# Feed-forward weights made beside the cross attentions, and transposed probabilities copied by halves of the keys

## The reference

```python
for layer in (0, 1):
    x = x + cross_attention(norm(x), ctx_1024, mask if layer == 0 else None)   # 16 heads of 16
    x = x + (linear_attention if layer == 0 else causal_attention)(norm(x))    # over the 64 latents
    x = x + (int8_ffn if layer == 0 else fp4_ffn)(norm(x))

def cross_attention(q, kv, mask):
    q, k, v = heads(q @ Wq.T + bq), heads(kv @ Wk.T + bk), heads(kv @ Wv.T + bv)
    p = softmax(q @ k.T / 4 + mask * -1e9)
    return merge(p @ v) @ Wo.T + bo

def ffn(x):                       # 256 -> 704 -> 256, weights quantised on the chip
    h = silu(quant(x) @ quant(w_gate).T) * (quant(x) @ quant(w_up).T)
    return quant(h) @ quant(w_down).T
# int8: weights by rows, w / (max|w| / 127) rounded; activations by one scale.
# fp4:  blocks of 16, w / (max|w| / 6) rounded to {0, .5, 1, 1.5, 2, 3, 4, 6}, times the scale.
```

## Time and profile before

| | |
|---|---|
| median of 3 runs | 1437.82 us (1437.0 to 1437.97) |
| the profiled execution | 1439.74 us, its span 1437.8 us |
| busy, of the span | PE 1300.0, PEld 895.3, DVE 939.4, ACT 784.8, POOL 656.6 us |
| mean granted TensorE clock | 0.955 of 2.4 GHz |

### The profile page before, as it was taken

How to read it: one execution, slowest core, us unless ns; L and a number is a source line. 1 busy time by engine, 2 the same in 40 slices (tenths; PEclk the granted TensorE clock), 3 DMA queues, 4 the chain that set the end, 5 groups by cost and what they waited for, 6 DMA issues and landing times. The chain is left out here.

```text
span 1437.8 us, 27154 instructions
## 1 busy us (share of the span) xinstructions
PE 1300.0 (90%) x10721; PEld 895.3 (62%) x10722; DVE 939.4 (65%) x1670; ACT 784.8 (55%) x1315; POOL 656.6 (46%) x351
## 2 busy tenths in 40 slices
PE   6999999999999966965599999999999997897697
PEld 3676676666666644642256666766667665696465
DVE  4656655666556755957657768676566566586886
ACT  4675666666666623534366666666666664354311
POOL 2755566656666522400145556565555555440200
PEclk9999999999999988987699999999999998899798
DMA  4221111211111030000210100200010000000000
GB/s 159 76 58 45 45 45 45 87 47 45 45 45 45 1 102 0 1 1 0 108 37 31 51 30 31 80 31 31 31 59 31 31 1 24 4 1 1 0 11 19
DMA packets 17085, 55.29 MB, mean 38 GB/s; under 512 B 2753, under 2 KB 8897, under 8 KB 12737
## 3 DMA queue, kind: packets, MB, share of 16 engines
q1 hardware_dynamic: 16960, 53.56, 11.4%
HBM read 52.51 MB, written 1.05 MB: 37 GB/s over the span
## 5 line engine op out<-in xcount | busy, mean ns | idle before, releaser
L429 POOL TENSOR_TENSOR ca_prob<-ca_prob,ca_inv_sum 128x1024 f32<-128x1024 f32 x256 | 493.4, 1948 | 378.4 <-DVE ca_inv_sum L707 378.4
L608 ACT ACTIVATE ca_kT<-bank,ca_bk 64x512 f32<-64x512 f32 x256 | 174.6, 682 | 223.4 <-PE bank L465 221.6
L512 PEld LDWEIGHTS bank<-ident,ca_prob 128*128 128x128 f32 x2048 | 238.4, 141 | 89.4 <-issue 65.7
L512 PE MATMUL bank<-ident,ca_prob 128*128 128x128 f32 x2048 | 266.7, 274 | 9.0 <-POOL ca_prob L429 7.0
L465 PE MATMUL bank<-ca_ctxT,ca_wk 128*128 128x512 f32 x512 | 244.4, 602 | 17.4 <-DMA ca_bk<-in_L_xattn_bk 17.4
L477 PE MATMUL bank<-ca_wv,ca_ctxT 128*128 128x256 f32 x1024 | 254.5, 392 | 0.0
L684 DVE CUSTOM_DVE_ANT_0 ca_neg_logit<-bank,ca_mask_add 128x1024 f32<-128x1024 f32 x128 | 151.6, 1222 | 131.6 <-PE bank L502 95.0
L477 PEld LDWEIGHTS bank<-ca_wv,ca_ctxT 128*128 128x128 f32 x1024 | 184.6, 190 | 82.2 <-issue 62.5
L687 DVE TENSOR_REDUCE ca_neg_max<-bank 128x1 f32<-128x1024 f32 x128 | 150.7, 1219 | 103.3 <-PE bank L502 103.3
L630 ACT ACTIVATE ca_prob<-ca_neg_logit,ca_neg_max 128x1024 f32<-128x1024 f32 x128 | 146.9, 1150 | 62.8 <-DVE ca_neg_max L684 62.8
L630 ACT ACTIVATE ca_prob<-bank,ca_neg_max 128x1024 f32<-128x1024 f32 x128 | 142.5, 1114 | 63.8 <-DVE ca_neg_max L687 63.8
(11 more groups left out here) (278 smaller groups left out, 1333.9 us busy)
## 6 DMA issues: line engine op xcount, KB each, us to landing
ca_ctxT<-in_ctxT SPq DMA_DIRECT2D x32, 1024.0 KB, 5.0
ca_mask_i<-in_mask SPq DMA_DIRECT2D x32, 256.0 KB, 6.4
lat<-in_x SPq DMA_DIRECT2D x1, 1024.0 KB, 4.9
out<-lat SPq DMA_DIRECT2D x8, 128.0 KB, 1.9
la_w_qkv<-in_L_attn_w_qkv SPq DMA_DIRECT2D x1, 768.0 KB, 3.9
la_w_down<-in_L_ffn_w_down SPq DMA_DIRECT2D x1, 704.0 KB, 8.0
ca_fw_raw<-in_L_ffn_w_down SPq DMA_DIRECT2D x1, 704.0 KB, 4.3
la_w_gate<-in_L_ffn_w_gate SPq DMA_DIRECT2D x1, 640.0 KB, 5.7
```

The costliest lines, as they stand in the source:

```text
L429: pool.tensor_tensor(prob[:, x, :], prob[:, x, :], inv_sum[:, x:x + 1].broadcast_to([P, CTX]), ALU.mult).then_inc(norm_ready, 1)
L512: tr = pe.transpose(bank[:, x, n * P:(n + 1) * P], prob[:, 2 * (s % 2) + p, (4 * h + n) * P:(4 * h + n + 1) * P], core.ident[:, :])
L608: op = act.activation(kT[half * S:(half + 1) * S, b % 2, 2 * m + r, :], bank[r * S:(r + 1) * S, x, :], ACT.Identity, bias=bk[r * S:(r + 1) ...
```

## The change

- **Copies by halves.** `take_t` becomes `take_t_on_vector(s - 1, 0)` and `take_t_on_scalar(s - 1, 1)`: VectorE copies half h = 0 of both pairs, ScalarE half h = 1 of both. The places in the lists stay.
- **Int8 weights in the first cross attention.** Raw weights are loaded one matrix at a time into one buffer. VectorE quantises each in five steps (from s = 4, 16, 28), TensorE transposes it in three units of four transposes (from s = 10, 22, 34), each into one bank of the pool, and ScalarE copies each unit out in two instructions. The linear attention loses that work, the int8 feed-forward its transposes and copies.
- **Fp4 weights in the second.** VectorE's eight steps start at s = 4, 20, 36 and leave the grid in f32 in the raw buffer, POOL multiplies by the scales at s = 12, 28, 44, TensorE transposes in units from s = 14, 30, 46, ScalarE copies. The fp4 feed-forward starts with the layer norm alone.
- **Memory and order.** q4 and attnT have half their size: the second half of the queries is projected at s = 28 and 29 in place of 8 and 12, when the first has been used, and attnT goes round over four batches. The mask is loaded into one buffer, not two, after the one before is converted. `queries` comes two steps later (s % 4 == 2). The bf16 identity is made before the first latents are transposed.
- The cross attention becomes a class `CrossAttention`, its plan of banks a class `Banks` with the same turn.

```diff
-        def take_t(eng, copy, s, p):
-            n = s // 2
-            j = 2 * (s % 2) + p
-            if n >= 2:
-                wait_filled(eng, ("pv", n - 2))
-            for h in range(2):
-                x = wait_filled(eng, ("t", s, p, h))
-                copy(probT[:, n % 2, 4 * h:4 * h + 4, j, :],
-                     bank[:, x, :].rearrange("p (n q) -> p n q", q=P)).then_inc(taken[x], 1)
+    def take_t_on_scalar(self, act, s, h):
+        n = s // 2
+        if n >= 2:
+            self.banks.wait_filled(act, ("pv", n - 2))
+        for p in range(2):
+            x = self.banks.wait_filled(act, ("t", s, p, h))
+            self.banks.free(act.activation(self.probT[:, n % 2, 4 * h:4 * h + 4, 2 * (s % 2) + p, :],
+                                           self.core.bank[:, x, :].rearrange("p (n q) -> p n q", q=P), ACT.Copy),
+                            ("t", s, p, h))
...
+class Banks:
+    def open(self, pe, key, bank=None):
+        if bank is None:
+            bank = 4 + self.turn % 4
+            self.turn += 1
+        wait(pe, self.taken[bank], self.count[bank])
+        self.count[bank] += 1
+        self.at[key] = (bank, self.count[bank])
+        return bank
...
 class Fp4Weights:
+    def scale_on_pool(self, pool, x):
+        pool.wait_ge(self.step, 8 * (x + 1))
+        grid, scale = fp4_scaled(self.raw[:, 0:self.blocks[x] * HD], self.scale[:, 0:self.blocks[x]], self.blocks[x])
+        pool.tensor_tensor(grid, grid, scale, ALU.mult).then_inc(self.scaled, 1)
+
+    def transposes_on_tensor(self, pe, x, i):
+        pe.wait_ge(self.scaled, x + 1)
+        b = self.banks.open(pe, ("w", x, i))
+        for c in (2 * i, 2 * i + 1):
+            r = self.ROWS[c]
+            for k in range(KD):
+                o = (c % 2 * KD + k) * P
+                if x < 2:
+                    tr = pe.transpose(self.core.bank[:, b, o:o + r], self.raw[0:r, c * D + k * P:c * D + (k + 1) * P],
+                                      self.core.ident[0:r, 0:r])
...
+class Int8Weights:
+    def step_on_vector(self, dve, x, n):
...
+        elif n == 3:
+            dve.wait_ge(self.step, 3 * x + 3)
+            for c in range(pieces):
+                dve.tensor_scalar(raw[:, c, :], raw[:, c, :], self.inv[:, c:c + 1], ROUND, ALU.mult, ALU.add)\
+                    .then_inc(self.rounded, 1)
+        else:
+            if x >= 1:
+                self.banks.wait_filled(dve, ("i", x - 1, self.UNITS - 1))
+            for c in range(pieces):
+                dve.wait_ge(self.rounded, first + c + 1)
+                dve.tensor_scalar(whole[:, c, :], raw[:, c, :], ROUND, None, ALU.subtract).then_inc(self.ready, 1)
...
+def first_layer(core, ffn_weights):          # second_cross alike, from FW_STEPS + 10
 (TensorE)
+                if 1 <= s <= STEPS:
+                    ca.transposes(pe, s - 1, 1)
+                for x in range(3):
+                    if 6 <= s - IW_STEPS[x] < 9:
+                        ffn_weights.transposes_on_tensor(pe, x, s - IW_STEPS[x] - 6)
+                if s in Q_STEPS:
+                    ca.project_q(pe, 1, Q_STEPS.index(s))
+                if s % 8 == 2 and s >= 10:
...
 (ScalarE)
+                if s < STEPS:
+                    ca.exponentials(act, s)
+                if s + 4 < STEPS:
+                    ca.take_k(act, s + 4)
+                if s >= 1:
+                    ca.take_t_on_scalar(act, s - 1, 1)
+                for x in range(3):
+                    if 6 <= s - IW_STEPS[x] < 9:
+                        ffn_weights.take_on_scalar(act, x, s - IW_STEPS[x] - 6)
...
 (VectorE)
+                if 1 <= s <= STEPS:
+                    ca.take_t_on_vector(dve, s - 1, 0)
+                if s < STEPS:
+                    ca.inverses(dve, s)
...
 (linear_attention, VectorE)
             ln.on_vector(dve)
-            ffn_weights.on_vector(dve)
             dve.wait_ge(w_loaded, 96)
...
 (fp4_ffn, POOL)
-            for x in range(3):
-                flat = wq[x][:, :, :].rearrange("p c n -> p (c n)").rearrange("p (n k) -> p n k", k=HD)
-                grid, scale = fp4_scaled(weights.grid[x][:, :], weights.scale[x][:, :], weights.blocks[x])
-                pool.tensor_tensor(flat, grid, scale, ALU.mult).then_inc(wq_ready, 1)
```

More of the change, by code:

```diff
@@ new lines, in take_on_scalar @@
+    def take_on_scalar(self, act, x, i):
+        b = self.banks.wait_filled(act, ("w", x, i))
+        for c in (2 * i, 2 * i + 1):
+            r = self.ROWS[c]
+            o = c % 2 * KD * P
+            if x < 2:
+                op = act.activation(self.wT[x][:, :, c * P:c * P + r],
+                                    self.core.bank[:, b, o:o + KD * P].rearrange("p (k q) -> p k q", q=P)[:, :, 0:r],
+                                    ACT.Copy)
+            else:
+                op = act.activation(self.wdT[0:r, c, :], self.core.bank[0:r, b, o:o + D], ACT.Copy)
+        self.banks.free(op, ("w", x, i))
@@ L242, with __init__ @@
 GROUPS = 4
 STEPS = B * GROUPS
-POOL_BANKS = (4, 5, 6, 7)
-Q_STEPS = (8, 12)
 HALF_CTX = CTX // 2
-class BankPlan:
-    def __init__(self):
-        self.uses = [0] * 8
+Q_STEPS = (28, 29)
+class Banks:
+    def __init__(self, core, sem):
+        self.core = core
+        self.filled = [sem(f"filled{n}") for n in range(8)]
+        self.taken = [sem(f"taken{n}") for n in range(8)]
+        self.count = [0] * 8
         self.at = {}
         self.turn = 0
[L257 to L263, removed]
@@ L298, in cross_attention, with done @@
[L298 to L303, removed]
+    def open(self, pe, key, bank=None):
[6 more added lines that the diff above has]
+        return bank
+    def done(self, instruction, key):
+        instruction.then_inc(self.filled[self.at[key][0]], 1)
@@ L304, in cross_attention @@
+IW_STEPS = (4, 16, 28)
+def first_layer(core, ffn_weights):
+    nc, d, bank = core.nc, core.dram, core.bank
     with ExitStack() as ctx:
         def sb(name, shape, dt=F32):
[L306 to L311, removed]
@@ L443, in _ @@
+            pool.wait_ge(ffn_weights.pad_set, 1)
+            pool.wait_ge(const_loaded, 64)
+            ca.queries(pool, 0)
+            ca.convert_mask(pool, 0)
+            ca.add_output_bias(pool)
             for s in range(STEPS):
-                normalise(s)
+                ca.normalise(pool, s)
                 if s % GROUPS == 0 and s // GROUPS + 1 < B:
-                    queries(s // GROUPS + 1)
-                    if masked:
-                        mask(s // GROUPS + 1)
-        @block.tensor
@@ new lines, in _ @@
+                    ca.convert_mask(pool, s // GROUPS + 1)
+                if s % GROUPS == 2 and s // GROUPS + 1 < B:
+                    ca.queries(pool, s // GROUPS + 1)
+        @block.scalar
+        def _(act):
+            ca.ln.on_scalar(act)
+            act.wait_ge(ca.wk_loaded, 32)
+            for n in range(4):
+                ca.take_k(act, n)
+            ca.take_latents_on_scalar(act)
+            act.wait_ge(ca.wq_loaded, 32)
+            ca.take_q_on_scalar(act, 0)
+            for s in range(STEPS + 1):
+                if s < STEPS:
+                    ca.exponentials(act, s)
+                if s + 4 < STEPS:
+                    ca.take_k(act, s + 4)
+                if s >= 1:
+                    ca.take_t_on_scalar(act, s - 1, 1)
+                for x in range(3):
+                    if 6 <= s - IW_STEPS[x] < 9:
+                        ffn_weights.take_on_scalar(act, x, s - IW_STEPS[x] - 6)
+                if s == Q_STEPS[0]:
+                    ca.take_q_on_scalar(act, 1)
@@ L1826, in _ @@
             down(TILES - 1)
-def cross(core, layer, ffn_weights=None):
-    with ExitStack() as ctx:
-        core.q4 = ctx.enter_context(core.nc.sbuf_tensor(f"q4_{layer}", [P, 4, B * S], F32))
-        core.attnT = ctx.enter_context(core.nc.sbuf_tensor(f"attnT{layer}", [P, KD, B * S], F32))
-        cross_attention(core, layer, layer == 0, layer == 0, ffn_weights)
 def perceiver(nc, dram, out):
```

1113 lines of the change are left out of this document (576 added, 537 removed).

## The result

| | before | after |
|---|---|---|
| median of 4 runs | 1437.41 us | 1529.66 us |
| lowest to highest | 1435.73 to 1437.97 | 1528.59 to 1531.32 |
| ratio, 95% interval | | 1.0642 [1.0629, 1.0655] |
| span of the profiled execution | 1437.8 | 1529.3 |

The change makes the kernel 92 us slower. The forecast was 1524, 5.7 us lower. The table gives the length of each stage, from the start of one layer norm to the next (rows L142), in the profiled executions. The third line has, for each stage, the forecast's terms.

A forecast was written before the change was run, and what follows sets the result against it. TensorE, full at 2.4 GHz in both cross attentions, was taken as the bound. Terms 75.1 + 6.8 + 3 + 4 + 10 - 8.4 - 4.0 = +86.5 on the profiled 1439.7, median 1.9 lower: 1524 us, range 1487 to 1552.

The forecast's parts named there:

- Copies by halves: Cross attentions: TensorE waits for ScalarE's t(p0,h1) copy behind take_k, 34 times 1.54 and 84 times 0.27 us: 75.1 us.
- the late inverse: Cross attention ends: VectorE's inverse, now behind a copy of the second transposes, delays POOL's normalisations: 3 us (1 to 6).
- rival A: Cross attentions: only the long bank waits bite, the 22.7 us of short ones go: 1490 us, chance 0.10.
- Weight units on TensorE: Both cross attentions: 36 weight transposes in each layer added to a full TensorE: 6.8 us (5 to 8).
- Ports in the second layer: Second cross attention: VectorE's two-input fp4 steps behind the inverse lengthen POOL's pair of normalisations: 4 us (0 to 7).
- Ports in the first layer: First cross attention: int8 steps of six short VectorE instructions beside POOL's normalisations: 10 us, between nothing and 19.
- Out of the linear attention: Linear attention: without 42 VectorE int8 weight instructions ahead of them, the first features run earlier: -8.4 us (-7 to -9).
- Out of the fp4 head: Fp4 feed-forward's layer norm: with POOL silent, L147 and L152 take 0.17 us each: -4.0 us (-3.5 to -4.2).
- B: Cross attentions: no bank wait, ScalarE's copy finishes before the next opener asks: 1434 us, faster, chance 0.07.
- C: Cross attentions: VectorE held by POOL in most weight steps, 19 us first layer, some 17 second: 1547 us, chance 0.13.
- D: Cross attentions: the copies balance but the ports don't, slower without a bank wait: 1449 us, chance 0.02.
- What was put at nothing: Half-size q4 and attnT, single mask buffer, later queries and weight loads, POOL's scale multiplications, early bf16 identity: no cost.

The follow-up runs named there:

- the fifth experiment: The changed kernel, halves kept, with each int8 rounding step one whole-width instruction in place of six: 1513.52 us, ratio 1.0532.
- pairs with one instruction: The changed kernel with copies by pairs again (VectorE pair 0, ScalarE pair 1) and int8 rounding steps as single instructions: 1430.96 us, ratio 0.9951.
- The third experiment: The changed kernel with ScalarE copying t(p1,h0's sibling) t(p1,h1) first and t(p0,h1) second: 1594.22 us, ratio 1.1092.
- the second experiment: The changed kernel, halves kept, with ScalarE copying t(p0,h1) before the key copies (take_k) and t(p1,h1) behind them: 1450.28 us, ratio 1.0101.
- the halves alone: The kernel before with only the copies split by halves, no weight work moved: 1503.48 us, ratio 1.0464.
- The last experiment: Pairs with one instruction, plus three POOL multiplications into an unread tile at the head of the fp4 feed-forward: 1438.61 us, ratio 1.0008.

## Why the prediction was right, point by point

The total is nearer than its parts. The first layer came out 8.4 us above its terms, the linear attention, int8 and fp4 stages together 4.9 below theirs, the causal attention 1.8 above. That these partly cancel is luck. The bounds 1508 to 1544 are also narrower than the terms' own bounds added up, which give some 1504 to 1549.

**Copies by halves (forecast 75.1): right in place, sort and size; the late inverse (3) right in place.** The cleanest measure is the difference between the fifth experiment and pairs with one instruction, in which nothing but the split differs: 1513.52 - 1430.96 = 82.6 us. The forecast has 75.1 + 3 + 4 = 82.1 for what hangs on it. Of that difference the waits for ScalarE's copies are 74.1 (70.1 - 2.8, and 34 x 0.2), those for POOL 2.0 (8.9 and 6.9). The rest is in no wait: TensorE's busy time, for the same 10722 matmuls, is 1301.8 against 1287.1, and without the loads' 6.8 that is 7.9 us of longer rows, not traced. So the large term is shown, and the other 7 only as a sum.

By stage it is 550.1 - 512.2 = 37.9 against 24.6 + 11.6 + 1.5 = 37.7 in the first, and 559.6 - 515.7 = 43.9 against 27.7 + 11.1 + 1.5 + 4 = 44.3 in the second. The third experiment shows that all the waits are there, the short ones too; that rules out rival A. The second shows that it is the order in one queue. The late inverse is seen in the halves alone, where the waits for POOL grew by 3.4 us (forecast 3). In the change they are 7.8, against 7.0 before: they stand at the stage ends, as said (4.0 between 500 and 573, 2.7 between 1240 and 1300), but nearer 1 us than 3 there.

**Weight units on TensorE (6.8): right,** 2.6 + 4.3 = 6.9 in pairs and one instruction.

**Ports in the second layer (4): nearer 2, and not shown apart.** The stage came out at +48.6 against +48.8, but the parts agree less well. In pairs and one instruction the second stage's +4.3 is no more than the units' 4.5. In the second experiment, where the bank waits are gone and the inverse is still late, it takes 518.8, +7.4: without the units 2.9 for the inverse and the ports together, where the forecast has 5.5. And in the halves alone the second layer loses 33.5 us and the first 30.8, with equal waits for ScalarE's copies; 2.7 is what the fp4 steps can have cost there. That the stage agrees to 0.2 is in part luck.

**Ports in the first layer (10, bounds 0 and 19): the term that was mis-sized.** From the stage's +58.4 the other terms take 24.6 + 11.6 + 2.3 + 1.5 = 40, which leaves 18.4; the fifth experiment took 17.9 off the stage.

It is the upper bound, and its mechanism was right: I had VectorE held for both normalisations and the maxima 4.8 late, and the trace has six instructions in 5.52 us and maxima 4.5 after the scores. Its sum was right partly by luck. It had six steps of six instructions, and the third matrix has two in each; and TensorE's waits for VectorE in this stage are 5.7 us for the value copy (L707) and 4.6 for the copy of the attention's output (L749), 9.6 more than before, not 19. Of the rest some 5 is the clock: it is 0.97 and 0.98 in the windows 60 to 160 and 160 to 260, and 1.00 in both in the fifth experiment.

Where I went wrong was in taking the middle between two rows. L177 in the earlier trace rows, which goes first and holds POOL, is a single long instruction; six short ones have five seams, and POOL came in at the first of them (99.19, behind a start at 99.02); the row that they are like is L147 in the earlier trace rows, where VectorE asks while POOL is busy. The Trainium skill, SBUF — State Buffer, section Who interferes with whom, says that VectorE and GpSimd lock the shared ports against each other for a whole instruction. These rows agree with it: the shortest of the fourteen L345 took 0.27 us and the longest 2.22, a little more than one of POOL's normalisations, and six together took 5.52, where one instruction takes 1.22 to 1.35.

With pairs in place the same edit gives only 521.1 - 512.2 = 8.9 us in this stage: some half of the 18 is the ports by themselves, and the other half comes only with halves. The bank waits are not what it needs, as the second experiment shows, which has six instructions and no bank waits. These are TensorE's waits for VectorE in the first layer there (60 to 500):

```profile
PE bank L598 <- DVE ca_v L707: 6.7, 3, 3.3
PE bank L537 <- DVE ca_attnT L749: 5.6, 4, 2.4
```

They are 12.3 us; in the changed kernel they are 10.3, with pairs 6.0 and in the fifth experiment 0.6. The stage takes 535.1 there, 14.0 more than with pairs. Its profiled execution was 7 us above the median of its runs, so up to 7 of the 14 could be that execution's own. What mainly differs from pairs there is the late inverse, behind VectorE's second copy; no run with six instructions moves the inverse alone.

**Out of the linear attention (-8.4): the mechanism right, the stage moved more.** The features after the change, with the map and the projection behind it (of before):

```profile
592.52 0.69 DVE L1207 TENSOR_TENSOR la_pre<-bank,la_b_map 128x512 f32<-128x512 f32 x1 [11.40 <-PE bank L1065]
...
595.68 1.05 PE L1065 MATMUL bank<-la_w_map,la_zT 128*128 128x128 f32 x8
...
599.14 2.21 PE L1089 MATMUL bank<-la_w_qkv,xnT 128*128 128x256 f32 x9 [0.69 <-ACT la_zT L1158]
```

VectorE is idle for 11.40 us ahead of the features; nothing stands before them. The value projection starts 599.14 - 573.6 = 25.5 us after the layer norm, where it was 549.88 - 515.2 = 34.7: -9.2. The other 1.2 us of the stage's -10.4 lie behind it, in code that the change doesn't touch. The same code varies by itself: in the halves alone, whose linear attention is that of the kernel before, the stage is 122.9 against 126.4, so the change's 116.0 is 6.9 to 10.4 less. The causal attention, which the change doesn't touch, is 113.8 there and 113.3 after the change, against 111.5. Stages with the same code differ by 2 to 3.5 us between kernels, and the stretches in which TensorE's granted clock is at half fall in other places. That these stretches are the cause was not tested.

**Out of the fp4 head (-4.0): right to the tenth, and incomplete.** After the change:

```profile
1430.28 0.17 DVE L147 TENSOR_SCALAR ff_var<-ff_mv 128x8 f32<-128x8 f32 x1
...
1430.96 0.17 DVE L152 TENSOR_TENSOR ff_fix<-ff_rstd 128x8 f32<-128x8 f32 x1
```

The first product of the stage (L1968) starts 19.2 us after the layer norm against 23.2 before. The last experiment, in which POOL multiplies beside the layer norm again, shows the cause: its first product starts 24.4 us after the layer norm does. Then 2.4 us more were gained. Windows of the stretch in which the products run, of the kernel before (1353 on) and after (1451 on), the same 24 us behind the head:

```profile
1353.00:1363.00 10.00, 10.00 (x31) 6.34 (x30) 6.99 (x10) 2.41 (x4) 0.00 (x0) 0.74 0.00 0
1363.00:1377.00 14.00, 12.03 (x41) 7.70 (x40) 11.85 (x17) 2.43 (x5) 0.00 (x0) 0.88 0.01 4
```

```profile
1443.00:1447.00 4.00, 2.75 (x10) 2.10 (x11) 3.83 (x6) 1.91 (x3) 0.00 (x0) 0.50 0.00 0
...
1451.00:1461.00 10.00, 8.02 (x35) 5.22 (x34) 8.02 (x12) 2.41 (x4) 0.00 (x0) 1.00 0.00 0
1461.00:1475.00 14.00, 14.00 (x60) 9.70 (x58) 12.16 (x20) 3.34 (x8) 0.00 (x0) 1.00 0.03 11
```

TensorE was at half clock when its activations came, as forecast, but returned to 2.4 GHz sooner: the granted clock is 1.00 where it had been 0.74 and 0.88. The last experiment has 0.75 in the first of these stretches again, so its layer norm, 5.2 us later, brings half of this back as well.

**The rivals.** A falls with the third experiment, B with the result. C gave 1547: its 19 us in the first layer are nearly there (18), its 17 in the second are not. The fp4 steps are single long instructions, which fits; no run tests it. D falls with the bank waits. What was put at nothing cost nothing that shows: in pairs and one instruction the cross attentions differ from before by the units' cost alone.

## What to carry to other kernels

When buffers rotate, a copy's place in its engine's queue is set by when its bank is asked for again, not by which engine has time: find for each opener the buffer so many places back, the engine that frees it, and what stands ahead of that copy. Here 0.27 us in a step of 7.4, and 1.54 in some, came to 74 us, while the idle engines had room for all of the copies. Work that is spread beside a full engine cost less here in few long instructions: cut in six, the last step of a conversion lasted as long as POOL's two normalisations and 1.4 us more, 5.52 in all, and as one instruction 1.35.

## What the runs showed beyond this

TensorE's granted clock fell to half inside a cross attention, which the kernel before doesn't show in its windows there. It came right behind the 3.91 us gap in the loads at 107.55:

```profile
107.00:108.60 1.60, 1.02 (x8) 0.83 (x8) 1.39 (x3) 1.57 (x3) 0.00 (x0) 1.00 0.96 220
108.60:112.00 3.40, 3.40 (x38) 1.73 (x40) 1.57 (x5) 1.98 (x4) 2.91 (x2) 0.51 0.25 55
112.00:116.00 4.00, 4.00 (x61) 3.55 (x54) 2.43 (x8) 2.38 (x4) 0.83 (x1) 0.99 0.00 0
```

For 3.4 us the clock is 0.51, at the lower level, and then 0.99 again; the work in it takes up to twice as long, so a stall of 3.1 us cost up to 1.7 more. With one instruction in place of six, the windows from 60 to 550 have 1.00 throughout. And work on POOL that nothing waits for cost 7.6 us, more than the 5.2 of the two small instructions that it held; by stages 1.2 of that stands behind the layer norm, where the lower clock lasted longer.
